# Fixed and range columns selected apart, the preparation in another order, block rows shared three to one

## The reference, cut to what matters

```python
x = x + attn_a(_layernorm(x), w_qkv, b_qkv, w_out, b_out)
x = x + ffn(_layernorm(x), gamma, beta, bases, slopes, oscale)
x = x + attn_b(_layernorm(x), ...)
x = x + ffn(_layernorm(x), gamma, beta, bases, slopes, oscale)
```

```python
onehot = tile_idx[None, :] == jnp.arange(NUM_TILES)[:, None]
tile_min = jnp.where(onehot, tok_min[None, :], jnp.inf).min(axis=1)
tile_max = jnp.where(onehot, tok_max[None, :], -jnp.inf).max(axis=1)
mn = tile_min[tile_idx][:, None]
mx = tile_max[tile_idx][:, None]
u = jnp.clip((x_slice - mn) / (mx - mn + 1e-08), 0.0, 1.0 - 1e-06)
b = spline_bases[tile_idx[:, None], j, gi]
s = spline_slopes[tile_idx[:, None], j, gi]
delta = (b + s * x_local) * output_scale[tile_idx][:, None]
```

## Time and profile before

| | |
|---|---|
| median of 3 runs | 3283.73 us (3281.1 to 3285.6) |
| profiled execution | 3282.32 us, span 3280.5 us, mean granted TensorE clock 0.951 |
| busy share of the span | PE 89%, DVE 76%, ACT 64%, POOL 55% |
| chain that ended last | PE 73%, DVE 12%, POOL 7% |

### The profile page before, as it was taken

One profiled execution on the slowest core, in us unless ns is written; L12 is line 12 of the kernel. 1 busy time (PEld: TensorE's weight loads), 2 busy tenths in 40 slices (PEclk: granted clock), 3 DMA queues, 4 the chain that ended last, 5 costly groups with the idle time before them and its releaser, 6 DMA issues.

```text
span 3280.5 us, 60794 instructions
## 1 busy us (share of the span) xinstructions
PE 2930.4 (89%) x19888; PEld 2424.4 (74%) x19888; DVE 2502.4 (76%) x6374; ACT 2093.4 (64%) x4556; POOL 1810.0 (55%) x1914
## 2 busy tenths in 40 slices
PE   5999999945769999999999999999999999977763
PEld 3777777734558888888888888888888888865652
DVE  4556666575658888888887887888888888889986
ACT  2556555523547777777777777777777777755531
POOL 1111111142677668676676767768676686766442
PEclk9999999957889999999999999999999999989985
DMA  2000000002566656656666566565666566543311
GB/s 94 1 0 0 0 0 0 1 28 87 160 189 193 187 173 172 203 161 191 189 173 198 151 201 200 157 196 173 189 188 178 175 179 194 165 128 92 103 34 52
DMA packets 572121, 422.74 MB, mean 129 GB/s; under 512 B 228691, under 2 KB 475219, under 8 KB 571734
## 3 DMA queue, kind: packets, MB, share of 16 engines
q1 hardware_dynamic: 571862, 419.51, 43.9%
HBM read 276.39 MB, written 143.01 MB: 128 GB/s over the span
## 4 chain that ended last, share of the span: by engine, by line
PE 73%; DVE 12%; POOL 7%; issue 3%; ACT 3%; DMA 1%; SPq 0%; POOLq 0%; DVEq 0%; ACTq 0%
PE bank L1999 25%; PE bank L2050 15%; PE bank L2147 6%; PE bank L1853 5%; POOL oT L812 4%; PE bank L2055 3%; PE bank L1828 3%; PE bank L1765 3%; PE bank L1838 3%; PE bank L2030 2%; PE bank L2038 1%; ACT oT L1099 1%; DVE acc L1546 1%; PE bank L1807 1%; PE bank L1823 1%
## 5 line engine op out<-in xcount | busy, mean ns | idle before, releaser
L779 POOL TENSOR_TENSOR acc<-acc,shifted 128x510 f32<-128x510 f32 x384 | 585.5, 1527 | 550.1 <-DVE acc L1546 546.9
L1546 DVE SCALAR_TENSOR_TENSOR acc<-bank,conv_w,acc 128x254 f32<-128x254 f32 (+1 forms) x1536 | 628.8, 471 | 98.8 <-ACT acc L1029 95.4
L1999 PE MATMUL bank<-x_k,w_kq 128*128 128x256 f32 x2048 | 504.0, 391 | 13.6 <-DMA x_k<-xT_scratch 9.4
L1027 ACT ACTIVATE shifted<-bank,conv_w 128x255 f32<-128x255 f32 x768 | 366.9, 478 | 218.5 <-issue 147.4
L1029 ACT ACTIVATE acc<-bank,conv_b,conv_w 128x256 f32<-128x256 f32 x768 | 439.8, 573 | 0.0
L1999 PEld LDWEIGHTS bank<-x_k,w_kq 128*128 128x128 f32 x2048 | 378.8, 194 | 81.3 <-issue 31.9
L796 POOL TENSOR_TENSOR inv<-inv,outer 128x30 f32<-128x30 f32 (+14 forms) x480 | 259.5, 541 | 37.6
L2147 PE MATMUL bank<-w_o,oT 128*128 128x256 f32 x1024 | 246.5, 385 | 33.4 <-POOL oT L812 33.4
L793 POOL TENSOR_TENSOR outer<-inv 128x30 f32<-128x30 f32 (+14 forms) x480 | 235.3, 490 | 30.3 <-DMA inv<-L_scratch 2.5
L2030 PE MATMUL bank<-kq 128*128 128x256 f32 x1024 | 244.4, 382 | 5.1 <-ACT kq L1039 4.0
L2147 PEld LDWEIGHTS bank<-w_o,oT 128*128 128x128 f32 x1024 | 190.7, 191 | 77.8 <-issue 52.1
(11 more groups left out here) (237 smaller groups left out, 6544.4 us busy)
## 6 DMA issues: line engine op xcount, KB each, us to landing
abc<-decay_scratch SPq DMA_DIRECT2D x64, 512.0 KB, 5.9
q_scratch<-kq SPq DMA_DIRECT2D x64, 512.0 KB, 6.8
L_scratch<-LM SPq DMA_DIRECT2D x64, 512.0 KB, 3.4
M_scratch<-LM SPq DMA_DIRECT2D x64, 512.0 KB, 6.6
LTm<-L_scratch SPq DMA_DIRECT2D x64, 512.0 KB, 4.5
MTm<-M_scratch SPq DMA_DIRECT2D x128, 256.0 KB, 4.3
kqm<-q_scratch SPq DMA_DIRECT2D x64, 512.0 KB, 4.3
k_scratch<-knw SPq DMA_DIRECT2D x64, 258.0 KB, 4.8
```

Source lines behind the costliest of these rows:

```text
L779: pool.tensor_tensor(dst, dst, shifted[:, u % 2, :, 1:], ALU.add).then_inc(Z["sumk" if u < 4 else "sumv"], 1)
L1027: act.activation(shifted[:, u % 2, i % 2, 1:], pj[:, 0:SEQ - 1], ACT.Copy, scale=conv_w[:, kind, bass.ds(head, 1), TAPS - 2:TAPS - 1].rear ...
L1546: dve.scalar_tensor_tensor(out=acc[:, kind, i, t:], in0=pj[:, 0:SEQ - t], scalar=wcol, in1=acc[:, kind, i, t:], op0=ALU.mult, op1=ALU.add) ...
L1999: mm = pe.matmul(dst[:, i * SEQ:(i + 1) * SEQ], w[:, k, head * DK:(head + 1) * DK], x[:, k, :], start=(k == 0), stop=(k == CT - 1))
```

## The change

1. **Preparation.** GpSimd increments only the 21 semaphores of `A` first; those of `R` and `Z` (124) come after `vx`. The bias split is its first work, the first power comes right after `maskd`. TensorE waits for 7 constants before the first transposes, and for the loads only behind them. ScalarE copies one column of `ident` as soon as it is there, and waits for all 13 constants after the first token copies. VectorE's moments of blocks 1, 2 and 3 go into `examined(0)`, `(1)` and `(3)` of `body(0)`, the wait for the second power to that body's end.

The diff, cut to its core:

```diff
@@ -646,10 +650,15 @@
...
-            for signals in (A, R, Z):
-                for signal in signals.values():
-                    pool.sem_inc(signal, 1)
+            for signal in A.values():
+                pool.sem_inc(signal, 1)
             ch = Chain(pool, p_step)
+            pool.wait_ge(loaded_bias, 32)
+            ch.link(pool.tensor_copy(bias_part[:, 0], bias[:]))
+            ch.link(pool.tensor_tensor(bias_rest[:], bias[:], bias_part[:, 0], ALU.subtract))
+            ch.link(pool.tensor_copy(bias_part[:, 1], bias_rest[:]))
+            ch.link(pool.tensor_tensor(bias_rest[:], bias_rest[:], bias_part[:, 1], ALU.subtract))
+            pool.tensor_copy(bias_part[:, 2], bias_rest[:]).then_inc(split_bias, 1)
@@ -662,22 +671,18 @@
...
                 pool.tensor_copy(maskd[:, i], maskb[:, P:]).then_inc(consts, 1)
+            pool.wait_ge(A["var"], past(1))
+            pool.wait_ge(consts, 3)
+            pool.tensor_tensor(rstd[:, 0:8], rstd[:, 0:8], half_neg[:, 0:8], ALU.pow).then_inc(A["rstd"], 1)
             pool.memset(rot[:], 0.0).then_inc(consts, 1)
             ch.link(pool.memset(q_scale[:], 0.0))
...
-            pool.wait_ge(loaded_bias, 32)
-            ch.link(pool.tensor_copy(bias_part[:, 0], bias[:]))
-            ch.link(pool.tensor_tensor(bias_rest[:], bias[:], bias_part[:, 0], ALU.subtract))
-            ch.link(pool.tensor_copy(bias_part[:, 1], bias_rest[:]))
-            ch.link(pool.tensor_tensor(bias_rest[:], bias_rest[:], bias_part[:, 1], ALU.subtract))
-            pool.tensor_copy(bias_part[:, 2], bias_rest[:]).then_inc(split_bias, 1)
-            n0 = ch.n
-            pool.wait_ge(A["var"], past(1))
-            pool.wait_ge(consts, 3)
-            pool.tensor_tensor(rstd[:, 0:8], rstd[:, 0:8], half_neg[:, 0:8], ALU.pow).then_inc(A["rstd"], 1)
+            for signals in (R, Z):
+                for signal in signals.values():
+                    pool.sem_inc(signal, 1)
@@ -895,7 +901,9 @@
...
             def start():
-                tokens(0), values_in(0), turned_in(0, 0), turned_in(0, 1)
+                tokens(0)
+                act.wait_ge(consts, 13)
+                values_in(0), turned_in(0, 0), turned_in(0, 1)
@@ -940,24 +948,39 @@
...
+                def ranges(half):
+                    act.wait_ge(R["selp"], past((FSTEPS + HALVES) * turn + (EARLY[turn] + 2 if half == 0 else FSTEPS + HALVES)))
+                    n = TILES // HALVES
+                    act.copy(T["selm"][:, half * n:(half + 1) * n, :], bank[6 + half][:, 0:2 * n].rearrange("p (i w) -> p i w", w=2)).then_inc(R["sel"], 1)
+
+                early = EARLY[turn]
+                turned(0)
+                for s in range(early):
+                    if s + 1 < early:
+                        turned(s + 1)
+                    fixed(s)
+                    if s == (1, 3)[turn]:
+                        last_signs()
+                turned(early), fixed(early)
+                ranges(0)
+                for s in range(early + 1, FSTEPS):
+                    turned(s), fixed(s)
+                ranges(1)
+
+            select(0, lambda: signs(tiles0, SEQS - 1, TPS))
@@ -1060,14 +1083,14 @@
                 def first_sweep(k):
                     act.wait_ge(Z["ap0"], past(3 * h + k + 1))
                     q = (k + 1) * BLK
-                    for i in range(HG // 2, HG):
+                    for i in range(HG // 2 if s < STEPS else 1, HG):
                         ins = act.copy(vn[hp][q:q + BLK, 0, i], bank[3][i * BLK:(i + 1) * BLK, 0:DK])
                     ins.then_inc(Z["z0"], 1)
@@ -1328,8 +1349,16 @@
...
                 def examined(part):
                     if first(b):
+                        if part == 0:
+                            dve.wait_ge(loaded_rest, 48)
+                            moments_of(1)
+                        if part == 1:
+                            moments_of(2)
                         if part == 2:
                             slope_signs()
+                        if part == 3:
+                            moments_of(3)
+                            dve.tensor_scalar(rstd[:, 8:], moments[:, 8:, 1], EPS, None, ALU.add).then_inc(A["var"], 1)
                         return
@@ -1371,18 +1398,16 @@
...
                 weighted_values(1)
+                if first(b):
+                    dve.wait_ge(A["rstd"], past(2))
             normalised(0)
-            dve.wait_ge(loaded_rest, 48)
-            moments_of(1, 3)
+            dve.wait_ge(consts, 13)
             dve.wait_ge(loaded_a, 80)
-            ch = Chain(dve, v_step, 6)
+            ch = Chain(dve, v_step, 0)
             def start():
                 rope(0, 0, ch), rope(0, 1, ch)
-                moments_of(2, 8)
-                moments_of(3, 11)
-                dve.tensor_scalar(rstd[:, 8:], moments[:, 8:, 1], EPS, None, ALU.add).then_inc(A["var"], 1)
@@ -1876,18 +1900,22 @@
...
             def start():
-                tokens(0), queries_keys(0, 0), queries_keys(0, 1), values_in(0), rotated(0, 0), rotated(0, 1)
+                tokens(0)
+                pe.wait_ge(loaded_a, 80)
+                queries_keys(0, 0), queries_keys(0, 1), values_in(0), rotated(0, 0), rotated(0, 1)
             sequences(pe, start, body)
             att_turned(SEQS - 1), project_att(SEQS - 1)
             def select(turn):
                 T = tiles[turn]
-                pe.wait_ge(R["pass1"], past(turn + 1))
-                for m, src in enumerate((T["run_min"], T["run_nmax"])):
-                    for i in range(FG):
-                        mm = pe.transpose(bank[3 + m][0:ROUTES, i * P:(i + 1) * P], src[:, i, :], ident[:])
-                    mm.then_inc(R["minT"], 1)
+                early = EARLY[turn]
+                if turn == 0:
+                    pe.wait_ge(A["res"], past(SEQS))
+                    pe.wait_ge(R["oh"], past(SEQS - 2))
+                else:
+                    pe.wait_ge(Z["res"], past(STEPS))
+                    pe.wait_ge(R["oh"], past(SEQS + len(DRAIN) - 2))
@@ -1896,19 +1924,40 @@
...
+                def fixed(s):
+                    pe.wait_ge(R["ohT"], past(FSTEPS * turn + s + 1))
+                    if s >= 2:
+                        pe.wait_ge(R["sel"], past((2 * FSTEPS + HALVES) * turn + 2 * (s - 1) + (s - 2 > early)))
+                    for i in range(FG):
+                        mm = pe.matmul(bank[2 + 2 * (s % 2) + i // 2][:, (i % 2) * 256:(i % 2) * 256 + FIXW], T["ohT"][:, s, i, :], table[:, 0:FIXW], start=True, stop=True)
+                    mm.then_inc(R["selp"], 1)
+
+                def extremes():
+                    pe.wait_ge(R["pass1"], past(turn + 1))
+                    for m, src in enumerate((T["run_min"], T["run_nmax"])):
+                        for i in range(FG):
+                            mm = pe.transpose(bank[6 + m][0:ROUTES, i * P:(i + 1) * P], src[:, i, :], ident[:])
+                        mm.then_inc(R["minT"], 1)
+
+                def ranges(half):
+                    pe.wait_ge(R["table"], past(turn + 1))
+                    n = TILES // HALVES
+                    for i in range(n):
+                        k = half * n + i
+                        mm = pe.matmul(bank[6 + half][:, 2 * i:2 * i + 2], T["ohT"][:, k // FG, k % FG, :], table[:, FIXW:TABW], start=True, stop=True)
+                    mm.then_inc(R["selp"], 1)
+
                 turned(0)
-                for s in range(FSTEPS):
-                    n = FSTEPS * turn + s
-                    if s + 1 < FSTEPS:
+                for s in range(early):
+                    if s + 1 < early:
                         turned(s + 1)
-                    pe.wait_ge(R["ohT"], past(n + 1))
-                    if s == 0:
-                        pe.wait_ge(R["table"], past(turn + 1))
-                    if s >= 2:
-                        pe.wait_ge(R["sel"], past(2 * (n - 1)))
-                    for i in range(FG):
-                        mm = pe.matmul(bank[2 + 2 * (s % 2) + i // 2][:, (i % 2) * 256:(i % 2) * 256 + TABW], T["ohT"][:, s % 2, i, :], table[:], start=True, stop=True)
-                    mm.then_inc(R["selp"], 1)
+                    fixed(s)
+                extremes()
+                turned(early), fixed(early)
+                ranges(0)
+                for s in range(early + 1, FSTEPS):
+                    turned(s), fixed(s)
+                ranges(1)
```

63 lines of the change are left out of this document (29 added, 34 removed).

## The result

The changed kernel takes 3266.42 us as a median of 5 runs (3258.79 to 3267.24), against 3283.73 us before (3281.01 to 3289.51). The ratio is 0.9942, 95% interval 0.9926 to 0.9957: faster by 14 to 24 us, where 33 were forecast as a median (32.3 by the sum). A second series gave 0.9936 (0.9920 to 0.9952). The profiled execution has a span of 3263.6 us, 16.9 under that of before. (`rsum` is the first instruction of the weighted values; each of the 16 sequences has two of them, its two halves.)

The account below looks back on a forecast made before the run. TensorE was taken to lead overall, with other engines binding at the four changed places, VectorE in the drain. -17.7 - 0.2 - 11.0 - 3.4 = -32.3 from 3282.32 gave 3250.0, as a median 3251 us, range 3245 to 3258.

Parts of the forecast that it names:

- Drain, -11.0: Drain, ten slots: VectorE copies one block row instead of two per sweep, saving 11.0 us, bounds -7 and -14.
- 1.77 a slot: Drain: six sweeps at 0.295 us saved on VectorE each, counted in full in slots 2, 4 and 5, 5.3 together.
- 1.6 each: Drain slots 6 and 7: VectorE's removed copies were to shorten each slot by 1.6 us, 3.2 together.
- the third rival: Drain gives nothing because hand-offs between TensorE and ScalarE bind: +11 us, 3262 as a median; chance 0.10.
- Preparation, -17.7: Kernel start: first row_min 19.4 us earlier, less 1.7 for displaced moments and the last wait; bounds -13 and -20.
- The blocks go elsewhere ... +1.6 ... The third ... nothing: First sequence: two moments blocks of 3.64 us into 5.70 of VectorE idle cost 1.6; the third, before the second rope, nothing.
- The fourth rival: Preparation gives only 12 us, as bias rows are late or displaced moments hold the first sequence: 3257; chance 0.05.
- First select, -0.2: First select: splines start 3.5 us earlier, but split range columns give it back on the second half; net -0.2.
- a rival with 1.5: Signs wait behind fixed copies, 1.5 us in first select, 2.1 in second, or pieces cost 0.26: 3255 to 3259; chance 0.12.
- Second select, -3.4: Second select: early steps finish by the extremes, then 12.7 us to the splines instead of 16.15, saving 3.4.

Follow-up runs that it names:

- the pair without the adds: Changed kernel with GpSimd's drain adds cut to 8 of 255 columns, block rows three to one and two to two: slot 7 differs by 1.03 us.

## Why the prediction was wrong

The sum had 32.3, the marks give 16.9. The difference is 15.4: 6.4 in the drain, 3.2 in the first sequence, 1.4 before the extremes, and 4.4 in two stretches that the change does not touch.

**Drain, -11.0, measured -4.6: the direction right, the price wrong. This is the step that failed most.** It is the reading that VectorE leads, so that its removed copies count in full or nearly: "1.77 a slot" in slots 2, 4 and 5 measured 0.9, 1.3 and 0.6, and "1.6 each" in 6 and 7 measured 1.0 and 1.0. Slot 3 gave 0.6 (0.9 forecast), slots 8 and 9 0.65 together (0.7). Slots 0 and 1 lost 1.03 and 0.52, where 0.9 and nothing were forecast. In slot 0 VectorE waits for a transfer of the stage before, 5.59 us in the kernel before and 7.38 in the changed one. What came last in place of VectorE is the chain over ScalarE's copies: that is the third rival, in which the hand-offs bind and for which 0.10 was given, and it is true by half. 31.93 of 33.00 busy said that VectorE led, not by how much. (That row is a window a little wider than its slot; the slot itself is 31.60 long, with 30.56 busy.) ScalarE had 14.75 idle in the slot, but not at the sweeps.

The profile of before had a short drain for its form: its ten slots took 318.0 us, in three other profiles with two to two and the adds whole 320.2 to 320.8. With three to one they took 311.1 to 315.8 over eleven, 313.4 in the mean. Against the mean of the four (319.9) the copies are worth 6.5 us, and the pair without the adds differs by 6.3.

**Preparation, -17.7: right at its own mark, wrong for what follows.** At the first weighted values it was 17.5. Part of that is luck: xn was late by 1.5 (2.21 beside GpSimd's memset), and the way from the first projection to `row_min` was taken too long by about as much (15 forecast, 13.2 measured from 17.08). The step that failed is "The blocks go elsewhere ... +1.6 ... The third ... nothing": it counted VectorE's time only. The blocks make ScalarE and then TensorE wait, TensorE's granted clock falls after that wait, and the first sequence's second half runs at 0.81. That is 3.2 us in the profile; over the eleven profiles the stretch is 1.4 to 6.0 longer than 16.84. The fourth rival had the displaced moments hold the first sequence, with 12 in place of 17.7 and a chance of 0.05.

**First select, -0.2: right** (0.17 gained from the extremes on), piece by piece. The signs, part of a rival with 1.5, did wait: 1.24 longer than before, most of the 1.4 lost ahead of the extremes. What was not seen is that before's 16.15 is one of two levels of the old form. The sum was made against the slower one.

**Second select, -3.4: right,** 3.7.

**Not in the sum:** 1.9 at the end of attention and 2.5 between the selects and the drain. From the last weighted values but one to the last it took 12.5 us in eleven profiles, all at clock 1.00, and 14.3 to 15.5 in seven, at 0.79 to 0.86. So the clock makes this difference; what brings it down there was not found. Of the 2.5, 2.1 lie between the first spline half and the first residual of the delta rule, a stretch of the same program that took 320.1 to 324.6 us over 18 profiles. The clock alone does not order these: 322.4 at 0.83 in the kernel before, 324.6 at 0.82 in the changed one, 320.1 at 0.82 with the third block moved. The cause stays open.

The range missed by 4 us because it treated its rivals as separate cases, one at a time. Here three of them came together, the hand-offs, the signs and the displaced moments, 6.4 + 1.4 + 3.2 = 11.0, and with them the 4.4 of the two open stretches.

## What to carry to other kernels

Work put into an engine's idle gap has two prices, its own time and the clock of the engine that waits behind it: moving VectorE work in front of a stretch in which TensorE is the bound can cost TensorE its full clock, so put it where VectorE itself waits, and look at the clock again. A busy share of 97% says who leads, not by how much; follow the chain of waits with the shortened operations and see which engine comes last next. Before summing against one profile, look in a second one whether a stretch has two levels.

## What the runs showed of the hardware

- TensorE's granted clock in a stretch differs between executions of one program: in the kernel before, the first select took 16.15 us at 0.50 in one profile and 11.02 at 0.85 in another, for the same 64 to 66 recorded matmuls. That makes 5 us in 3280.
- A wait of TensorE of 1.36 us stood before the fall of its clock in eleven of eleven profiles that have blocks behind the second and third group of minima; in the two where that wait is gone, the clock stayed at 1.00 until the second weighted values.
- Back-to-back pairs of a 128-column weight load and a 2-column float32 matmul were 0.21 us apart at clock 0.50 (32 in 6.82 us) and about 0.10 apart at 0.92.
- VectorE's scaling of two 128 x 256 tiles took 2.21 us beside a GpSimd memset of 1.80 that began 0.09 before, and 0.74 without. The first of the two scalings lasted 1.90, until 0.19 behind the memset's end, the second 0.40. The Trainium skill ("SBUF — State Buffer", "SBUF: two separate sides") says that GpSimd and a VectorE operation in a two-port mode share a port pair, which whoever starts first holds for its whole instruction while the other is blocked; the row agrees.
